# Graph layer with gated update: the second edge bias added by VectorE out of PSUM, the low half taken from SBUF, and x + h summed by GpSimd

## The chip, the core and the metric

The kernel runs on one core of a Trainium2 chip. The metric is the device time of one execution in microseconds. The core has a matrix engine (PE, with its weight loads shown apart as PEld), VectorE (DVE), ScalarE (ACT), GpSimd (POOL) and SyncE (SP). Each of them takes its own instructions strictly in program order; between engines there are only semaphores.

## The reference

`x` is 100000 x 128 (nodes), and there are 50000 edges, sorted by destination, each of one of 4 types.

```python
h = relu(layernorm(x))                                  # per row
for each edge e = (src, dst, t):
    hid = relu(concat(h[src], h[dst]) @ W1[t] + b1[t])  # 256 -> 128
    m   = hid @ W2[t] + b2[t]                           # 128 -> 128, the second edge bias is b2
agg = segment_sum(m, dst)                               # 100000 x 128
gi, gh = agg @ W_ih.T + b_ih, h @ W_hh.T + b_hh         # 3 x 128 each
r, z = sigmoid(i_r + h_r), sigmoid(i_z + h_z)
n = tanh(i_n + r * h_n)
out = x + (1 - z) * n + z * h
```

## The kernel before, in words

The nodes go in 196 groups of 512 rows (128 partitions x 512 columns in the transposed form), the edges in 204 units of 256. One loop of steps, unrolled by 8, does in each step one stage of several units and several groups, so that the work of a step belongs to some ten different units and groups. Every engine has its own function `step(i, m)`, and the order of the calls in it is the order of the instructions on that engine: it is written out by hand. In the steady part each step handles one group of nodes and one unit of edges on every engine.

What a step does around the change:

- **Edges.** POOL gathers the rows of x for both ends (`e_x`, four indirect DMAs a step, L593). ACT normalises them, PE transposes them and multiplies by W1 into bank BE1 (L1455, L1456), ACT adds b1 and applies relu (`e_r`, L1303). PE then makes the messages in the other half of BE1: first a product of a matrix of ones with `b2_rows` (L1468, 256 columns), which puts b2 there, and onto it the two products with W2 (L1472). ACT copies the messages rounded to fp32r into the high half of `e_msg` (L1324, at the end of its step), DVE subtracts that from the bank and writes the low half (`low_half`, L1078), and ACT issues the store of both halves to `messages` in DRAM (`store_messages`, L1251). SP loads windows of 64 message rows for a group of nodes (`n_win`, L544) when the unit five after the group's number has been stored.
- **Sums.** POOL makes the windows' tags relative to the group (`n_rel`, L644), DVE makes selection matrices from them (`n_sel`, L1099), and PE sums the messages with these (L1444).
- **Gates.** PE's products of three passes each (L1364, L1365, L1366) give r, z and n for the group: in a step the products of r (six passes), then those of h_n (three passes into bank BHN), transposes, sums and edges, then those of i_n (three passes), then those of z (six passes), then the messages (L1468, L1472), then four transposes of `n_e` of the group before into bank BHN (L1482). ACT computes `n_r` (L1274), `n_n` (L1311) and `n_zc`, which is 1 - z (L1317, behind the products of z).
- **Output.** DVE forms `n_d` (L1143) and `n_e` (L1150, waits for `n_zc`), PE transposes `n_e` back into BHN, and DVE forms `n_out` (L1088) from bank BHN and `n_xh`. `n_xh` is x + h, made by DVE from `n_h` and `n_x` (L1117).

Three orders matter. On DVE, a step ends with `n_d` and `n_e`, and the next one begins with `n_out`, then `low_half`, then `n_sel`. On PE, the h_n products overwrite bank BHN, which `n_out` reads:

```python
gate(BRZ, 0, s, "ha").then_inc(n_gate_r, 1)
if due(g - 1):
    pe.wait_ge(n_outed, g - 1)
...
gate(BHN, 2, s, "h").then_inc(n_gate_hn, 1)
```

On POOL, a step waits until ACT has normalised an older unit (`e_normed`), moves a word to keep the order (`gate_word`, L599), and issues two gathers, `n_rel` and two gathers; in every fourth step `n_rel` comes ahead of `gate_word`. Steps 20 to 116 have list writes too (L579), three in every fourth step.

Of the kernel before, what the change touches and what calls it, by code (L numbers as in the profile page):

```python
# [12 lines left out]
P = 128  # L13
D = 128
# [75 lines left out]
def gnn_layer(nc, x, edge_rows, dst_cols, dst_flat, types, W1, b1, W2, b2, WihT, WhhT, b_ih, b_hh, out):  # L90
# [22 lines left out]
    with ctx:  # L113
# [30 lines left out]
        b2_rows = sb("b2_rows", [P, TYPES * D], F32R)  # L144
        row_is = sb("row_is", [P, 2])
# [72 lines left out]
        def borrow(buffer, at, width):  # L218
# [18 lines left out]
        b2_two, b2_hi, b2_lo, b2_parts = (  # L237
            e_msg[:].rearrange("p r t w -> p (r t w)")[:, at * TYPES * D:(at + 1) * TYPES * D] for at in range(4))
        b2_two, b2_parts = b2_two.bitcast(F32), b2_parts.bitcast(F32)
# [142 lines left out]
        e_high = sem("e_high")  # L382
        e_low = sem("e_low")
# [172 lines left out]
        def _(pool):  # L556
# [90 lines left out]

            def half_of(i):
# [5 lines left out]
            def step(i, m):  # L654
# [12 lines left out]
                if m % 4 != 2:  # L667
                    relative_tags(i - LAG + 1, m - LAG + 1)
                if within(i, UNITS):
                    gather(i, m, (1,))  # L670
# [16 lines left out]
        def _(dve):  # L687
# [386 lines left out]
            def low_half(i, m):  # L1074
                q, s = i - 10, (m - 10) % UNROLL
                if within(q, UNITS):
                    dve.wait_ge(e_high, q + 1)
                    V.tensor_tensor(e_msg[:, s, :, D:2 * D],  # L1078
                                    bank[BE1][:, message_part].rearrange("p (t d) -> p t d", t=2),
                                    e_msg[:, s, :, 0:D].bitcast(F32), ALU.subtract).then_inc(e_low, 1)  # L1080

            def step(i, m):
                g, s = i - LAG - 2, (m - LAG - 2) % 4
                if within(g, NG):
                    dve.wait_ge(n_back, g + 1)
                    if due(g - 3):
                        dve.wait_ge(n_stored[s], uses(g - 4, s, 4, 16))
                    V.tensor_tensor(n_out[:, s, :], n_xh[:, s, :], bank[BHN][:], ALU.subtract).then_inc(n_outed, 1)  # L1088
                in_head = isinstance(i, int) and i < LAG - 2
                if not in_head:  # L1090
                    low_half(i, m)
                ln_part(i, m, 0)
                g, s = i - LAG + 1, (m - LAG + 1) % 4
                if within(g, NG):
# [5 lines left out]
                    ins.then_inc(n_seled, 1)  # L1100
                ln_part(i, m, 1)
# [13 lines left out]
                if within(g, NG):  # L1115
                    dve.wait_ge(n_normed, g + 1)
                    V.tensor_tensor(n_xh[:, s % 4, :], n_h[:, s % 2, :], n_x[:, s, :], ALU.add).then_inc(n_xhed, 1)  # L1117
# [48 lines left out]
                if isinstance(i, int) and i == CHECK_STEP:  # L1166
                    check_inputs()
                if isinstance(i, int) and i == GENERAL_STEP:
                    general_sums()

# [18 lines left out]
        def _(act):  # L1189
# [77 lines left out]
            def step(i, m):  # L1267
                normalise_edges(i, m, (0, 1))
                g, s = i - LAG, (m - LAG) % 2
# [5 lines left out]
                store_messages(i, m)  # L1275
# [20 lines left out]
                if within(q, UNITS):  # L1296
# [7 lines left out]
                    last.then_inc(e_relued, 1)  # L1304
                g, s = i - LAG, (m - LAG) % 2
# [14 lines left out]
                q, s = i - 9, (m - 9) % UNROLL  # L1320
                if within(q, UNITS):
                    act.wait_ge(e_messaged, q + 1)
# [209 lines left out]
```

## Time and profile before

| | us |
|---|---|
| median of 3 runs | 1748.21 (1745.63 to 1748.54) |
| the profiled execution's own time | 1746.99 |
| its span, first to last instruction | 1745.1 |
| PE busy | 1618.8 (93% of the span) |
| DVE busy | 1645.1 (94%) |
| ACT busy | 1455.9 (83%) |
| POOL busy | 1015.6 (58%) |

The profile is that of one execution. Of matmuls the ends are modelled, so that the start of one to the start of the next says more than a duration. The granted PE clock is 1.000 over the whole span. A row's "idle before, releaser" names what ended the engine's last wait.

### The profile page before, as it was taken

How to read it: one execution, taken by the hardware profiler on the slowest of the kernel's cores; microseconds unless marked ns; L12 is line 12 of the kernel's file. 1: busy time of each engine (PE TensorE's matmuls, PEld its weight loads, DVE VectorE, ACT ScalarE, POOL GpSimd, SP SyncE). 2: the span in 40 equal slices, each digit the busy share in tenths (PEclk: the TensorE clock that was granted, in tenths of full speed). 3: DMA queues.
4: the chain of work that ended last, by engine and by line, in shares of the span. 5: the costliest groups of instructions: out<-in, count | busy, mean ns of one | idle time of the engine just before them, and what ended most of it. 6: DMA issues, size and time to landing. Idle time of an engine off the chain costs nothing.

```text
span 1745.1 us, 43079 instructions
## 1 busy us (share of the span) xinstructions
PE 1618.8 (93%) x10182; PEld 1422.8 (82%) x10182; DVE 1645.1 (94%) x4809; ACT 1455.9 (83%) x3401; POOL 1015.6 (58%) x1343
## 2 busy tenths in 40 slices
PE   0236999999999999999999999999999999999998
PEld 0225888888888888888888888888888888888887
DVE  8997999999999999999999999999999999999986
ACT  0025999999898999999999999999999999999896
POOL 5745666666666666766666555555555655565500
PEclk9999999999999999999999999999999999999999
DMA  2224777777777777777777777777777777777653
GB/s 84 68 61 137 193 203 199 202 199 201 197 203 203 198 201 198 200 199 198 199 197 202 194 199 195 198 197 200 195 202 195 199 199 195 202 192 200 191 142 100
DMA packets 477561, 319.97 MB, mean 183 GB/s; under 512 B 106541, under 2 KB 463629, under 8 KB 477454
## 3 DMA queue, kind: packets, MB, share of 16 engines
q10 hardware_dynamic: 261792, 156.12, 29.1%
q1 hardware_dynamic: 186542, 107.39, 26.2%
q0 software_dynamic: 29120, 55.33, 13.1%
q8 instruction: 30, 0.49, 0.1%
q14 instruction: 77, 0.63, 0.1%
HBM read 212.05 MB, written 106.98 MB: 183 GB/s over the span
## 4 chain that ended last, share of the span: by engine, by line
PE 74%; ACT 0%; issue 0%; DVE 0%; ACTq 0%; DVEq 0%
PE bank L1364 14%; PE bank L1366 13%; PE bank L1365 13%; PE bank L1444 9%; PE bank L1456 4%; PE bank L1472 4%; PE bank L1455 4%; PE bank L1482 4%; PE bank L1434 4%; PE bank L1426 4%; PE bank L1468 1%; ACT n_zc L1317 0%; ACT n_r L1274 0%; DVE n_out L1088 0%; ACT n_h L1226 0%
## 5 line engine op out<-in xcount | busy, mean ns | idle before, releaser
L593 POOL DMA_INDIRECT e_x<-in_x,rows_now x816 | 821.4, 1007 | 247.2 <-issue 239.0
L1209 ACT ACTIVATE e_h<-e_x,shift,rstd 128x128 f32<-128x128 f32 x816 | 355.4, 485 | 103.3 <-DVE shift L1071 65.1
L1226 ACT ACTIVATE n_h<-n_x,shift,rstd 128x128 f32<-128x128 f32 x784 | 385.8, 492 | 0.0
L1364 PE MATMUL bank<-n_h_hi,whh_hi 128*128 128x512 f32 x588 | 248.8, 423 | 1.7 <-ACT n_zc L1317 1.2
L1364 PE MATMUL bank<-n_a_hi,wih_hi 128*128 128x512 f32 x588 | 246.9, 420 | 1.3 <-DVE bank L1111 1.3
L1444 PE MATMUL bank<-n_sel,n_win 128*128 128x256 f32 x1568 | 235.4, 292 | 0.5 <-DVE n_sel L1099 0.5
L1366 PE MATMUL bank<-n_a_hi,wih_lo 128*128 128x512 f32 x588 | 231.9, 394 | 0.0
L1366 PE MATMUL bank<-n_h_hi,whh_lo 128*128 128x512 f32 x588 | 231.7, 394 | 0.0
L1365 PE MATMUL bank<-n_h_lo,whh_hi 128*128 128x512 f32 x588 | 231.5, 394 | 0.0
L1099 DVE TENSOR_SCALAR n_sel<-iota,n_rel 128x256 fp32r<-128x256 f32 x784 | 230.0, 356 | 0.2 <-POOL n_rel L644 0.2
L1365 PE MATMUL bank<-n_a_lo,wih_hi 128*128 128x512 f32 x588 | 229.6, 390 | 0.0
L1274 ACT ACTIVATE n_r<-bank,bsum 128x512 f32<-128x512 f32 x196 | 135.1, 689 | 79.5 <-PE bank L1366 73.7
L1444 PEld LDWEIGHTS bank<-n_sel,n_win 128*128 128x128 f32 x1568 | 198.9, 189 | 2.5 <-DVE n_sel L1099 0.9
L1455 PE MATMUL bank<-e_ht,w 128*128 128x128 f32 x816 | 162.3, 281 | 34.0 <-DVE e_msg L1078 34.0
L1317 ACT ACTIVATE n_zc<-bank,bneg 128x512 f32<-128x512 f32 x196 | 134.8, 688 | 63.5 <-PE bank L1366 53.1
L599 POOL TENSOR_TENSOR gate_word<-g_power 1x1 f32<-1x1 f32 x224 | 46.4, 207 | 228.2 <-issue 107.1
L644 POOL TENSOR_TENSOR n_rel<-n_win,base 128x4 f32<-128x4 f32 x196 | 54.5, 278 | 203.0 <-DMA n_win<-messages 134.6
L1150 DVE TENSOR_TENSOR n_e<-n_d,n_zc 128x512 f32<-128x512 f32 x196 | 135.8, 693 | 37.2 <-ACT n_zc L1317 29.5
L1456 PE MATMUL bank<-e_ht,w 128*128 128x128 f32 x816 | 162.2, 281 | 0.0
L1143 DVE TENSOR_TENSOR n_d<-bank,n_n 128x512 f32<-128x512 f32 x196 | 134.8, 688 | 27.0 <-ACT n_n L1311 23.3
L1455 PEld LDWEIGHTS bank<-e_ht,w 128*128 128x128 f32 x816 | 128.3, 196 | 36.6 <-issue 36.6
L1004 DVE BATCH_NORM_STATS2 bn<-e_x 128x6 f32<-128x256 f32 x408 | 155.1, 421 | 0.0
(179 smaller groups left out, 3842.5 us busy)
## 6 DMA issues: line engine op xcount, KB each, us to landing
n_win<-messages SPq DMA_DIRECT2D x1568, 64.2 KB
messages<-e_msg ACTq DMA_DIRECT2D x204, 257.0 KB, 3.0
n_x<-in_x ACTq DMA_DIRECT2D x195, 256.0 KB
out<-n_out ACTq DMA_DIRECT2D x195, 256.0 KB
e_x<-in_x,rows_now POOLq DMA_INDIRECT x816
rows_now<-lists SPq DMA_DIRECT2D x204, 2.0 KB
lists<-picks,list_rows POOLq DMA_INDIRECT x72
w<-in_W SPq DMA_DIRECT2D x1, 512.0 KB, 5.1
```

The costliest lines, as they stand in the source:

```text
L593: G.indirect_dma_start(e_x[:, s, 2 * end + t, :], None, x, bass.IndirectOffsetOnAxis(ap=rows_now[:, s, t, end:end + 1], axis=0)).then_inc( ...
L1004: return V.bn_stats(bn[:, slot, col:col + 2, :].rearrange("p k c -> p (k c)"), rows.rearrange("p t d -> p d t"))
L1099: ins = V.tensor_scalar(n_sel[:, s % 2, k, :], iota[:], n_rel[:, s % 2, k:k + 1], None, ALU.is_equal)
L1150: V.tensor_tensor(n_e[:, s, :], n_d[:, s, :], n_zc[:, s, :], ALU.mult).then_inc(n_eed, 1)
L1209: last = A.activation(e_h[:, s % 2, k, :], e_x[:, s, k, :], ACT.Relu, scale=rstd[:, slot, col + k:col + k + 1], bias=shift[:, slot, col + ...
L1226: last = A.activation(n_h[:, s % 2, cols], n_x[:, s, cols], ACT.Relu, scale=rstd[:, slot, col + 4 + k:col + 5 + k], bias=shift[:, slot, co ...
L1364: T.matmul(o, w_hi, v_hi, start=start, stop=False, skip_group_check=onto)
L1365: T.matmul(o, w_hi, v_lo, start=False, stop=False, skip_group_check=onto)
L1366: return T.matmul(o, w_lo, v_hi, start=False, stop=stop, skip_group_check=onto)
L1444: last = T.matmul(o, n_win[:, w, k, part_ * D:(part_ + 1) * D], n_sel[:, s, k, :], start=n == 0, stop=n == 3)
L1455: T.matmul(o, w1[:, kind, 0, :], e_ht[:, s, t * P:(t + 1) * P], start=True, stop=False)
L1456: last = T.matmul(o, w1[:, kind, 1, :], e_ht[:, s, (2 + t) * P:(3 + t) * P], start=False, stop=True)
```

## The change

Four things are changed, and the results are the same up to rounding.

1. PE no longer multiplies ones with `b2_rows`; its two products with W2 start the bank themselves.
2. DVE gets an operation `biased` at the end of its step: bank BE1 plus the bias (kept in the new SBUF buffer `b2_two`) into the low half of `e_msg`, in fp32. ACT's copy to the high half reads that buffer in place of the bank and stands later, in the next step behind the first two tiles of `normalise_edges`; DVE's `low_half` now reads SBUF alone and stands behind `n_sel`. The products of the next unit into BE1 wait for `biased` in place of `low_half`.
3. ACT issues the store of the messages behind the relu of the hidden part in place of ahead of `normalise_edges(i, m, (2, 3))`.
4. `n_xh` is made by POOL (`node_sum`), behind `n_rel` in the odd half of the step's gathers, in place of DVE.

```diff
+        b2_two = sb("b2_two", [P, TYPES * D])
...
+            def node_sum(g, m):
+                s = m % UNROLL
+                if not within(g, NG):
+                    return
+                if isinstance(g, int) and g == 0:
+                    pool.wait_ge(n_seled, 1)
+                pool.wait_ge(n_normed, g + 1)
+                if due(g - 3):
+                    pool.wait_ge(n_outed, g - 3)
+                G.tensor_tensor(n_xh[:, s % 4, :], n_h[:, s % 2, :], n_x[:, s, :], ALU.add).then_inc(n_xhed, 1)
...
                 if m % 4 != 2:
                     relative_tags(i - LAG + 1, m - LAG + 1)
+                node_sum(i - LAG + 1, m - LAG + 1)
                 if within(i, UNITS):
                     gather(i, m, (1,))
...
                     dve.wait_ge(e_high, q + 1)
-                    V.tensor_tensor(e_msg[:, s, :, D:2 * D],
-                                    bank[BE1][:, message_part].rearrange("p (t d) -> p t d", t=2),
+                    V.tensor_tensor(e_msg[:, s, :, D:2 * D], e_msg[:, s, :, D:2 * D].bitcast(F32),
                                     e_msg[:, s, :, 0:D].bitcast(F32), ALU.subtract).then_inc(e_low, 1)
...
                     dve.wait_ge(n_back, g + 1)
+                    dve.wait_ge(n_xhed, g + 1)
...
-                if within(g, NG):
-                    dve.wait_ge(n_normed, g + 1)
-                    V.tensor_tensor(n_xh[:, s % 4, :], n_h[:, s % 2, :], n_x[:, s, :], ALU.add).then_inc(n_xhed, 1)
...
+                biased(i, m)
...
+            def biased(i, m):
+                q, s = i - 9, (m - 9) % UNROLL
+                if within(q, UNITS):
+                    dve.wait_ge(e_messaged, q + 1)
+                    first = 2 * ((m - 9) % 2)
+                    V.tensor_tensor(e_msg[:, s, :, D:2 * D].bitcast(F32),
+                                    bank[BE1][:, message_part].rearrange("p (t d) -> p t d", t=2),
+                                    b2_two[:, first * D:(first + 2) * D].rearrange("p (t d) -> p t d", t=2),
+                                    ALU.add).then_inc(e_biased, 1)
...
+                q, s = i - 10, (m - 10) % UNROLL
+                if within(q, UNITS):
+                    act.wait_ge(e_biased, q + 1)
+                    act.wait_ge(e_tagged, q + 1)
+                    A.activation(e_msg[:, s, :, 0:D], e_msg[:, s, :, D:2 * D].bitcast(F32), ACT.Copy).then_inc(e_high, 1)
...
-                store_messages(i, m)
                 normalise_edges(i, m, (2, 3))
...
                     last.then_inc(e_relued, 1)
+                store_messages(i, m)
...
                     if due(q):
-                        pe.wait_ge(e_low, q)
+                        pe.wait_ge(e_biased, q)
...
-                    T.matmul(bank[BE1][:, message_part], ones_r[:], b2_rows[:, first * D:(first + 2) * D],
-                             start=True, stop=False)
                     for t in range(2):
                         o = bank[BE1][:, 2 * P + t * D:2 * P + (t + 1) * D]
-                        last = T.matmul(o, e_r[:, s, t * P:(t + 1) * P], w2[:, first + t, :], start=False, stop=t == 1)
+                        last = T.matmul(o, e_r[:, s, t * P:(t + 1) * P], w2[:, first + t, :], start=True, stop=True)
```

How the instructions stand on DVE from the end of one step into the next, before (the names in brackets are the semaphores waited for; `root` rows are the small steps of the inverse square root, in some steps there and in some not):

```order
L1143 TENSOR_TENSOR n_d<-bank,n_n 128x512 [waits n_ned]
L1150 TENSOR_TENSOR n_e<-n_d,n_zc 128x512 [waits n_back,n_ded,n_zed]
L1061 TENSOR_SCALAR root<-half_var 128x32 [waits ln_vared]
L1088 TENSOR_TENSOR n_out<-n_xh,bank 128x512 [waits n_stored1,n_back]
L1078 TENSOR_TENSOR e_msg<-bank,e_msg 128x2x128 [waits e_high]
L1027 TENSOR_TENSOR root_t<-root 128x32 [waits ln_ops]
L1099 TENSOR_SCALAR n_sel<-iota,n_rel 128x256 [waits n_summed,n_reled]
```

And the same place of the changed kernel, where L1188 is `biased` and L1092 `low_half`:

```order
L1154 TENSOR_TENSOR n_d<-bank,n_n 128x512 [waits n_ned]
L1161 TENSOR_TENSOR n_e<-n_d,n_zc 128x512 [waits n_back,n_ded,n_zed]
L1075 TENSOR_SCALAR root<-half_var 128x32 [waits ln_vared]
L1188 TENSOR_TENSOR e_msg<-bank,b_two 128x2x128 [waits e_messaged]
L1102 TENSOR_TENSOR n_out<-n_xh,bank 128x512 [waits n_stored1,n_xhed,n_back]
L1041 TENSOR_TENSOR root_t<-root 128x32 [waits ln_ops]
L1111 TENSOR_SCALAR n_sel<-iota,n_rel 128x256 [waits n_summed,n_reled]
L1111 TENSOR_SCALAR n_sel<-iota,n_rel 128x256 x3
L1092 TENSOR_TENSOR e_msg<-e_msg 128x2x128 [waits e_high]
```

`biased` now stands between `n_e` and `n_out`, and `low_half` has gone behind `n_sel`.

On PE the messages and what follows them, of the changed kernel (L1491 are the products with W2, L1501 the transposes of `n_e`, L1385 to L1387 the passes of a gate). One row, the product with ones ahead of L1491, is gone; the wait for `n_outed` stands where it stood:

```order
L1387 MATMUL bank<-n_a_hi,wih_lo 128x512
L1491 MATMUL bank<-w,e_r 128x128 [waits e_relued]
L1491 MATMUL bank<-w,e_r 128x128
L1501 MATMUL bank<-ident,n_e 128x128 [waits n_ted,n_eed]
L1501 MATMUL bank<-ident,n_e 128x128 x3
L1385 MATMUL bank<-n_h_hi,whh_hi 128x512 [waits n_zed,n_alo,n_hlo]
...
L1385 MATMUL bank<-n_h_hi,whh_hi 128x512 [waits n_outed]
```

On POOL one step of the changed kernel reads as follows (L659 is `node_sum`); before, the row L659 is not there and the others stand the same:

```order
L601 TENSOR_TENSOR gate_word<-g_power 1x1 [waits l_gated,e_normed,l_loaded1]
L595 DMA e_x<-in_x,rows_now 128x128 x2
L646 TENSOR_TENSOR n_rel<-n_win,base 128x4 [waits n_seled,n_windowed0]
L659 TENSOR_TENSOR n_xh<-n_h,n_x 128x512 [waits n_outed,n_normed]
L595 DMA e_x<-in_x,rows_now 128x128 x2
```

## Rows read from the trace of the kernel before

**Rows 1.** The page: busy time and share of span; the chain that ended last.

```profile
PE 1618.8 (93%) x10182; PEld 1422.8 (82%) x10182; DVE 1645.1 (94%) x4809; ACT 1455.9 (83%) x3401; POOL 1015.6 (58%) x1343
...
PE 74%; ACT 0%; issue 0%; DVE 0%; ACTq 0%; DVEq 0%
```

**Rows 2.** Who waited for whom: us in total, times, longest us.

```profile
ACT n_zc L1317 <- PE bank L1366: 53.1, 156, 0.7
...
DVE n_e L1150 <- ACT n_zc L1317: 29.5, 89, 0.7
...
PEld bank L1364 <- DVE n_out L1088: 9.4, 45, 0.8
```

**Rows 3.** Timeline, one steady step: start us, duration us, engine, line, what.

```profile
1005.35 0.39 PE L1364 MATMUL bank<-n_h_hi,whh_hi 128*128 128x512 f32 x1
...
1010.60 0.39 PE L1366 MATMUL bank<-n_a_hi,wih_lo 128*128 128x512 f32 x1
...
1010.83 0.28 PE L1468 MATMUL bank<-b_rows,ones_r 128*128 128x256 f32 x1
...
1010.95 0.60 PE L1472 MATMUL bank<-w,e_r 128*128 128x128 f32 x4
...
1011.03 0.69 ACT L1317 ACTIVATE n_zc<-bank,bneg 128x512 f32<-128x512 f32 x1 [0.27 <-PE bank L1366]
...
1011.79 0.70 DVE L1150 TENSOR_TENSOR n_e<-n_d,n_zc 128x512 f32<-128x512 f32 x1
...
1012.41 0.68 DVE L1088 TENSOR_TENSOR n_out<-n_xh,bank 128x512 f32<-128x512 f32 x1
...
1013.01 0.41 DVE L1078 TENSOR_TENSOR e_msg<-bank,e_msg 128x256 fp32r<-128x256 f32 x1
...
1013.09 0.39 PE L1366 MATMUL bank<-n_a_hi,wih_lo 128*128 128x512 f32 x1
...
1013.14 0.19 PEld L1364 LDWEIGHTS bank<-n_h_hi,whh_hi 128*128 128x128 f32 x1
...
1013.32 0.39 PE L1364 MATMUL bank<-n_h_hi,whh_hi 128*128 128x512 f32 x1
...
1013.34 1.13 DVE L1099 TENSOR_SCALAR n_sel<-iota,n_rel 128x256 fp32r<-128x256 f32 x4
```

**Rows 4.** Groups by line, DVE: count, busy us, mean ns, idle before.

```profile
L1078 DVE TENSOR_TENSOR e_msg<-bank,e_msg 128x256 fp32r<-128x256 f32 x204 | 85.1, 417 | 9.0 <-ACT e_msg L1324 9.0
```

**Rows 5.** Timeline, POOL's part of the same step.

```profile
1007.24 0.18 POOL L599 TENSOR_TENSOR gate_word<-g_power 1x1 f32<-1x1 f32 x1 [1.49 <-ACT e_h L1209]
...
1010.14 0.21 POOL L644 TENSOR_TENSOR n_rel<-n_win,base 128x4 f32<-128x4 f32 x1
...
1011.77 0.95 POOL L593 DMA_INDIRECT e_x<-in_x,rows_now  x1 [0.31 <-issue]
```

**Rows 6.** Groups by line, POOL: gathers, list writes, and its two wide operations.

```profile
L593 POOL DMA_INDIRECT e_x<-in_x,rows_now x816 | 821.4, 1007 | 247.2 <-issue 239.0 <-DMA n_win<-messages 0.6 <-POOL gate_word L599 0.3
...
L579 POOL DMA_INDIRECT lists<-picks,list_rows x72 | 71.3, 990 | 22.0 <-issue 22.0
...
L560 POOL IOTA n_xh<- 128x816 int32 x1 | 2.2, 2175 | 0.0
L568 POOL IOTA n_x<- 128x512 int32 x1 | 0.5, 544 | 0.0
```

**Rows 7.** Timeline: POOL's word and DVE's sum of two SBUF operands.

```profile
1000.12 0.68 DVE L1117 TENSOR_TENSOR n_xh<-n_h,n_x 128x512 f32<-128x512 f32 x1
1000.12 0.76 POOL L599 TENSOR_TENSOR gate_word<-g_power 1x1 f32<-1x1 f32 x1
```

**Rows 8.** Timeline: store of messages, the windows loaded behind it, and the relu.

```profile
1005.69 0.45 ACTq L1251 DMA_DIRECT2D messages<-e_msg  x1
...
1009.09 5.03 SPq L544 DMA_DIRECT2D n_win<-messages  x8
...
1009.18 0.62 ACT L1303 ACTIVATE e_r<-bank,b_cols 128x128 f32<-128x128 f32 x2
```

More of the change, by code:

```diff
@@ L235, in gnn_layer @@
         descends = borrow(n_zc[:], 0, ECOLS)
-        b2_two, b2_hi, b2_lo, b2_parts = (
-            e_msg[:].rearrange("p r t w -> p (r t w)")[:, at * TYPES * D:(at + 1) * TYPES * D] for at in range(4))
-        b2_two, b2_parts = b2_two.bitcast(F32), b2_parts.bitcast(F32)
+        b2_hi, b2_lo, b2_parts = (
+            e_msg[:].rearrange("p r t w -> p (r t w)")[:, at * TYPES * D:(at + 1) * TYPES * D] for at in range(3))
+        b2_parts = b2_parts.bitcast(F32)
         ends = n_d[:].rearrange("p r w -> p (r w)").bitcast(I32).rearrange("p (k e c) -> p k e c", k=SEGMENTS, e=2)
@@ L382, in gnn_layer @@
         e_high = sem("e_high")
+        e_biased = sem("e_biased")
         e_low = sem("e_low")
@@ L1089, in step @@
                 in_head = isinstance(i, int) and i < LAG - 2
-                if not in_head:
-                    low_half(i, m)
                 ln_part(i, m, 0)
@@ L1100, in step @@
                     ins.then_inc(n_seled, 1)
+                if not in_head:
+                    low_half(i, m)
                 ln_part(i, m, 1)
@@ L1319, in step @@
                 normalise_nodes(i, m, (3,))
-                q, s = i - 9, (m - 9) % UNROLL
-                if within(q, UNITS):
-                    act.wait_ge(e_messaged, q + 1)
-                    act.wait_ge(e_tagged, q + 1)
-                    A.activation(e_msg[:, s, :, 0:D], bank[BE1][:, message_part].rearrange("p (t d) -> p t d", t=2),
-                                 ACT.Copy).then_inc(e_high, 1)
             pipeline(nc, act, LAST, LOOP_END, step)
```

## The prediction

> **What bounds the kernel now.** The page comes first: PE is busy for 93% of the span, DVE for 94%, and the chain that ended last runs over PE for 74% of it [rows 1]. Two engines as full as that leave little room between them, so the list of waits comes next, for those near PE. ACT's `n_zc` waited for the products of z in 156 of 196 groups, DVE's `n_e` waited for `n_zc` in 89, and the weight load of a gate product waited for DVE's `n_out` in 45 [rows 2]. That is a ring: PE, ACT, DVE and PE again. So the last view is the timeline of one steady step, read from one start of the h_n products to the next [rows 3].
>
> The reader is to see that two paths lead from the last pass of z (1010.60) to the next h_n products (1013.32), and that they are equally long. The first is PE's own stream: the bias product at 1010.83, the messages from 1010.95, transposes, six passes of r of which the last starts at 1013.09, and 0.23 us behind it the h_n product, the distance at which a pass follows any other (1010.60 to 1010.83). PE does not pause. The second goes through the other engines: `n_zc` starts 0.43 us after the last pass of z and takes 0.69, `n_e` starts 0.07 after its end, `n_out` 0.62 after the start of `n_e`, takes 0.68, and the weight load of the h_n product starts 0.05 after that (1013.14), 0.18 ahead of the product. The load came right behind `n_out`; it had been held by it. With the 5.25 us from 1005.35 to 1010.60, which belong to both, the second ring is 5.25 + 0.43 + 0.69 + 0.07 + 0.62 + 0.68 + 0.05 + 0.18 = 7.97 us, and a step of PE is 7.97 us too. `n_out` needs the transposes on PE and `n_xh`, but not `n_e`: that it follows `n_e` is DVE's order alone.
>
> **The change part by part.**
>
> *The bias product is removed from PE.* The next product starts 0.12 us behind it (1010.83 to 1010.95) [rows 3], and there are 204 units [rows 4]: 24 us of PE's stream. But it lies between the two ends of the ring's second path, so it shortens the first path alone. If the second is longer, PE reaches the h_n products 0.12 us sooner and waits there. I cost it at nothing; what hides it is the term that follows, and without that it would be worth the 24 us.
>
> *`biased` is added to DVE between `n_e` and `n_out`.* Before, nothing but a small root step stood there. Its nearest row is the old `low_half`, which also reads 256 columns of the bank and as many of SBUF: 0.417 us each [rows 4], but the instruction behind it starts 0.33 us after it (1013.01 to 1013.34) [rows 3], since consecutive instructions overlap. So `n_out` comes 0.33 us later (0.33 to 0.42). It does not wait for the messages on top: their products begin 0.23 us after the last pass of z, while `n_e` is not done before 1.8 us after it. Queued behind it are `n_out` and `n_sel`, and PE waits for both; the first is next. What can be recovered is part of the 0.07 ahead of `n_e`, because DVE reaches it earlier without `n_xh`, and of the 0.18 between load and product: at least 0, at most 0.25 together. A weight load lasts 0.19, which speaks for little room in the 0.18, and a wait for a semaphore must remain of the 0.07, so I take 0.06. That makes a step 0.27 us longer (0.08 to 0.42). Steps 19 to 212 have both a unit whose messages are due and an h_n product behind: 194 x 0.27 = 52 us (16 to 81).
>
> *`n_xh` leaves DVE.* An instruction of 512 columns takes a place of 0.60 us there (1012.41 to 1013.01) [rows 3]; against it stands 0.33 for `biased`, so DVE has 0.27 us a step less to do. It stood between `n_sel` and `n_d`, where DVE will now wait for `n_n` and `n_zc` instead. Worth nothing while `n_e` follows `n_zc`, as it nearly does already.
>
> *`low_half` moves behind `n_sel`, ACT's copy to the next step, the store behind the relu.* `n_sel` follows `n_out` 0.33 us sooner, which cancels the lateness of `n_out` for the sums on PE. The copy stands ahead of `n_r`, whose products end some 0.2 us after the copy can: nothing. The store goes from 1005.69 to the relu's end near 1009.8, and the windows start 3.4 us behind a store and take 5.03 to issue (1009.09) [rows 8]: from about 1013 to 1018. Granting them 3.4 us to land, they are there near 1020.9, and `n_sel` asks for their tags at 1013.34 + 7.97 = 1021.3, later still with longer steps. Nothing, with half a microsecond to spare; beyond that each microsecond would be one of DVE's.
>
> *`n_xh` comes to POOL.* No row shows a wide sum on POOL. From below bounds it a plain fill of 512 columns, 0.54 us; from above the patterned fill of 816 columns, 2.18 us, which for 512 is 1.37 [rows 6]. A sum passes over two operands, each at no more than the plain fill's speed, so I take 1.2. POOL's step runs from 1007.24 to 1012.72 [rows 5], 5.8 us with the usual gap of 0.3 behind it; three list writes in every fourth step of 20 to 116 add 3 x (0.99 + 0.3) / 4 = 1.0 [rows 6]. With the sum that is 7.0, or 8.0 in the steps with lists, against 8.24 for the new ring. It fits, barely.
>
> The Trainium skill speaks against this move: its page "GPSIMD Engine Reference", section "4.1 Engine selection", gives wide sums to VectorE, as GpSimd is about twice as slow with two inputs. By the 4497 ns it states for 2048 columns the sum would be about 1.1 us, an estimate, and the total the same.
>
> *The two engines collide.* POOL's one-element word, which takes 0.18 us [rows 5], took 0.76 when it started with DVE's `n_xh`, and ended 0.08 after it [rows 7]: POOL was held while DVE read two operands from SBUF. The reverse, a long POOL sum holding DVE, has no row. The operations it could hold are `low_half` (now of two SBUF operands), the small root steps, and `n_e`. Where POOL waits for `n_normed`, `n_e` is already running. For the others, 1.2 of 8.24 us is a chance of 15% of a hold of 0.6 us on average, 0.09 a step or 17 us in all; from 0, if the wait on PE covers it, I take 8.
>
> The Trainium skill's page "SBUF — State Buffer", section "Who interferes with whom", states this as a lock: VectorE with two SBUF inputs against a GpSimd instruction that reads SBUF, and whichever comes second is blocked to the end. Rows 7 agree for one direction; by the page the 17 us would stand, and without its other direction 0.
>
> **Sum.** 1746.99 (the profiled execution, whose span is 1745.1 with 1.9 around it) + 52 + 8 = 1807. The median of the runs is 1.2 above that execution, so 1808.
>
> **The rivals.**
>
> *The second path has room after all (faster).* Then the step is PE's own, 0.12 us shorter: 1748 - 24 = 1724. For it speaks that DVE gets 0.27 us a step back and that PE's own recorded wait is tiny. It decides where `n_out` can end 0.27 us sooner than I have it, and the only way is an earlier `n_e`. Against it: `n_zc` starts a fixed 0.43 after PE, and `n_e` starts 0.07 after that is done, so freed DVE time ahead of `n_e` has nothing to start.
>
> *POOL becomes the bound (slower still).* With a sum of 1.4 us, held for 0.7 by `n_e` (the row of 0.70), and waiting in order for the late windows, POOL's step with lists comes to 8.0 + 0.2 + 0.7 = 8.9 us. Its 97 steps would cost 97 x (8.9 - 8.24) = 64 us more: 1872. For it speaks how full POOL is in that part; against it, that POOL's waits can overlap with these holds, and that a longer ring gives it room.
>
> *Nothing measurable* would need losses of exactly the size of a gain; I see no mechanism that fixes it there.
>
> **How the numbers follow.** The forecast has a chance of 0.76, with a range of its own of 1764 (0.08 a step, no collisions) to 1846 (0.42 and 17). The faster rival gets 0.10, POOL 0.11, no change 0.03. The range that leaves out no more than two in ten is 1770 to 1848. About 0.2% (3.5 us) is what can be told from no change: faster 0.10, same 0.03, slower 0.87.
>
> **What the profile of the changed kernel would show.** Right: PE waits for `n_out` ahead of the h_n products in nearly every step, some 0.4 us each (0.27 and the 0.12 of the product that is gone), and the step is about 8.24; `biased` takes about 0.42 and `n_out` starts some 0.95 after `n_e`; `n_e` waits for `n_zc` nearly always; DVE's busy time falls by about 45 us (0.68 less, 0.42 more a step) while the span grows. Wrong: PE without waits there and steps of 7.85 (the first rival), or steps of 20 to 116 longer than those behind them with DVE waiting for `n_rel` (the second). Long root steps or a long `low_half` would show the collision.

## The result, and the profile after it

The changed kernel takes 1985.65 us in the median of its runs (1981.04 to 1990.93), beside 1746.92 us for the kernel before (1744.72 to 1748.54). The ratio is 1.1368, with a 95% interval of 1.1336 to 1.1401: it is slower by 239 us. The forecast was 1808 us and the range 1770 to 1848, so the sign was right and the size was not. The profiled execution has a span of 1989.1 us.

The page of the changed kernel, its span and its line of busy times, which answers to [rows 1]:

```profile
span 1989.1 us, 43203 instructions
...
PE 1713.2 (86%) x9978; PEld 1417.4 (71%) x9978; DVE 1782.7 (90%) x4817; ACT 1522.0 (77%) x3401; POOL 1231.7 (62%) x1539
```

DVE was to lose about 45 us of work and its busy time went up by 138. That is the first sign that DVE's instructions are being held: the same instructions take longer. The groups of instructions on DVE and POOL show which (busy us, mean ns of one, idle ahead of them and for whom):

```profile
L1111 DVE TENSOR_SCALAR n_sel<-iota,n_rel 128x256 fp32r<-128x256 f32 x784 | 340.1, 493 | 59.8 <-POOL n_rel L646 57.5 <-issue 2.3
L1161 DVE TENSOR_TENSOR n_e<-n_d,n_zc 128x512 f32<-128x512 f32 x196 | 135.9, 694 | 62.0 <-ACT n_zc L1344 56.8
L1188 DVE TENSOR_TENSOR e_msg<-bank,b_two 128x256 f32<-128x256 f32 x204 | 87.7, 430 | 2.8 <-PE bank L1491 2.6 <-issue 0.2
L1047 DVE TENSOR_TENSOR root<-root_t,root 128x32 f32<-128x32 f32 x104 | 40.9, 393 | 1.9
...
L659 POOL TENSOR_TENSOR n_xh<-n_h,n_x 128x512 f32<-128x512 f32 x196 | 262.1, 1337 | 103.7 <-ACT n_h L1248 98.8 <-issue 2.4 <-DVE n_sel L1111 1.3
```

In the kernel before, the mean of `n_sel` is 356 ns, 230.0 us in all, and that of this root operation 193. `n_e` is as it was (694 after, 693 before), and `biased` takes 430. POOL's sum takes 1337 ns, where the prediction had 1200.

The list of waits, the answer to [rows 2]:

```profile
POOL n_rel L646 <- DMA n_win<-messages: 265.6, 103, 6.9
ACT n_a_hi L1318 <- PE bank L1465: 129.5, 88, 6.0
PEld bank L1465 <- DVE n_sel L1111: 128.1, 90, 5.3
PEld bank L1385 <- DVE n_out L1102: 116.5, 194, 1.8
POOL n_xh L659 <- ACT n_h L1248: 98.8, 62, 4.5
...
DVE n_sel L1111 <- POOL n_rel L646: 57.5, 53, 4.7
```

The wait for `n_out` now stands in 194 steps, as forecast for the ring. But ahead of it stands a chain that the prediction did not have: `n_rel` waits for the windows, `n_sel` for `n_rel`, PE's sums (L1465) for `n_sel`, and ACT's `n_a_hi` for PE. POOL's wait for the windows does no harm by itself: it was 135 us in 38 steps of the kernel before, where `n_sel` waited for `n_rel` once, for 0.2 us. The wait that tells is that of `n_sel`, here 57.5 us in 53 steps.

Counted from the starts of `n_zc` in the trace, the steps of the kernel before are alike (median 7.98 us, one of 195 over 8.5). Of the changed kernel's, 81 are under 8.5 and 52 over 9.5, up to 12.6. A short step, from one `n_zc` to the next (answers to [rows 3]):

```profile
1206.62 0.69 ACT L1344 ACTIVATE n_zc<-bank,bneg 128x512 f32<-128x512 f32 x1 [0.40 <-PE bank L1387]
1207.34 0.69 DVE L1161 TENSOR_TENSOR n_e<-n_d,n_zc 128x512 f32<-128x512 f32 x1 [0.39 <-ACT n_zc L1344]
1207.95 0.42 DVE L1188 TENSOR_TENSOR e_msg<-bank,b_two 128x256 f32<-128x256 f32 x1
1208.28 0.68 DVE L1102 TENSOR_TENSOR n_out<-n_xh,bank 128x512 f32<-128x512 f32 x1
1209.01 0.19 PEld L1385 LDWEIGHTS bank<-n_h_hi,whh_hi 128*128 128x128 f32 x1 [0.43 <-DVE n_out L1102]
...
1214.82 0.69 ACT L1344 ACTIVATE n_zc<-bank,bneg 128x512 f32<-128x512 f32 x1 [0.30 <-PE bank L1387]
```

This is the predicted ring to the tenth: `n_out` starts 0.94 us after `n_e` (forecast 0.95), the weight load has waited 0.43 (forecast 0.4), the step is 8.20 (forecast 8.24). The missing time is in the long steps. Three kinds of them stand out, and one excerpt of each carries the rest of this document.

**W, a window that lands late.** Same trace: store, windows behind it, and what waits for them.

```profile
1204.68 0.42 ACTq L1273 DMA_DIRECT2D messages<-e_msg  x1
1208.70 5.13 SPq L546 DMA_DIRECT2D n_win<-messages  x8
...
1217.34 0.20 POOL L646 TENSOR_TENSOR n_rel<-n_win,base 128x4 f32<-128x4 f32 x1 [3.09 <-DMA n_win<-messages]
1217.58 2.53 DVE L1111 TENSOR_SCALAR n_sel<-iota,n_rel 128x256 fp32r<-128x256 f32 x4 [0.22 <-POOL n_rel L646]
1217.61 1.28 POOL L659 TENSOR_TENSOR n_xh<-n_h,n_x 128x512 f32<-128x512 f32 x1
1220.16 1.21 PE L1465 MATMUL bank<-n_sel,n_win 128*128 128x256 f32 x8 [1.02 <-DVE n_sel L1111]
```

`n_sel` itself is only 0.22 us late here. But POOL stands in `n_rel` until the windows land, and its next instruction is the sum, which then starts with `n_sel`. The four of `n_sel` take 2.53 us in place of 1.13 [rows 3], and PE waits.

**L, the sum on the root operation.** In two of four steps a root operation stands between `n_e` and `biased`:

```profile
1044.15 0.69 DVE L1161 TENSOR_TENSOR n_e<-n_d,n_zc 128x512 f32<-128x512 f32 x1 [0.62 <-ACT n_zc L1344]
1044.58 1.42 POOL L659 TENSOR_TENSOR n_xh<-n_h,n_x 128x512 f32<-128x512 f32 x1 [1.53 <-ACT n_h L1248]
1044.76 1.29 DVE L1047 TENSOR_TENSOR root<-root_t,root 128x32 f32<-128x32 f32 x1
1045.98 0.41 DVE L1188 TENSOR_TENSOR e_msg<-bank,b_two 128x256 f32<-128x256 f32 x1
```

The sum waits for ACT's `n_h` and so starts while `n_e` runs. `n_e` keeps its 0.69; the small operation behind it takes 1.29 in place of 0.19, and ends with the sum (1046.05 and 1046.00). `biased` and `n_out` are behind it. In the changed kernel 22 of the 96 root operations at this place are held (over 0.6 us), since late windows shift POOL in many steps; in e4 below, with the windows in time, 60 of 96.

**P, a step with list writes on POOL.** POOL's work and `n_sel`:

```profile
1031.30 0.69 ACT L1344 ACTIVATE n_zc<-bank,bneg 128x512 f32<-128x512 f32 x1 [0.40 <-PE bank L1387]
...
1034.90 0.21 POOL L646 TENSOR_TENSOR n_rel<-n_win,base 128x4 f32<-128x4 f32 x1
1035.06 1.27 POOL L659 TENSOR_TENSOR n_xh<-n_h,n_x 128x512 f32<-128x512 f32 x1
1035.15 2.40 DVE L1111 TENSOR_SCALAR n_sel<-iota,n_rel 128x256 fp32r<-128x256 f32 x4 [1.32 <-POOL n_rel L646]
...
1037.61 1.67 PE L1465 MATMUL bank<-n_sel,n_win 128*128 128x256 f32 x8 [1.98 <-DVE n_sel L1111]
...
1043.43 0.69 ACT L1344 ACTIVATE n_zc<-bank,bneg 128x512 f32<-128x512 f32 x1 [0.71 <-PE bank L1387]
```

Here no window is waited for. POOL comes to `n_rel` late from its three list writes, `n_sel` waits 1.32 for it and is then held by the sum as well, and the step takes 12.13 us. Part of that is PE's clock: its granted share was 0.50, the lower of its two levels (1.2 GHz of 2.4), from 1038.5 to 1041.0, right behind its wait of 1.98 us, and 1.00 in a later stretch (1250 to 1280). The eight products of the sums take 1.67 us here and 1.21 in the excerpt of W.

### The profile page after: what moved, and what is told of

Its sections match the earlier page's. It is cut to its first block and busy times, and to the rows that moved or that the text cites. A ratio compares the mean times of both kernels' runs of the same rounds, so it can differ in the third digit from the quotient of the medians.

```text
span 1989.1 us, 43203 instructions
## 1 busy us (share of the span) xinstructions
PE 1713.2 (86%) x9978; PEld 1417.4 (71%) x9978; DVE 1782.7 (90%) x4817; ACT 1522.0 (77%) x3401; POOL 1231.7 (62%) x1539
## 5 line engine op out<-in xcount | busy, mean ns | idle before, releaser
L595 POOL DMA_INDIRECT e_x<-in_x,rows_now x816 | 790.6, 969 | 208.3 <-issue 170.2
L1111 DVE TENSOR_SCALAR n_sel<-iota,n_rel 128x256 fp32r<-128x256 f32 x784 | 340.1, 493 | 59.8 <-POOL n_rel L646 57.5
L1465 PE MATMUL bank<-n_sel,n_win 128*128 128x256 f32 x1568 | 243.1, 299 | 107.2 <-DVE n_sel L1111 106.2
L659 POOL TENSOR_TENSOR n_xh<-n_h,n_x 128x512 f32<-128x512 f32 x196 | 262.1, 1337 | 103.7 <-ACT n_h L1248 98.8
L1385 PE MATMUL bank<-n_h_hi,whh_hi 128*128 128x512 f32 x588 | 270.1, 459 | 38.1 <-DVE n_out L1102 33.0
L1465 PEld LDWEIGHTS bank<-n_sel,n_win 128*128 128x128 f32 x1568 | 203.8, 194 | 129.2 <-DVE n_sel L1111 128.1
L646 POOL TENSOR_TENSOR n_rel<-n_win,base 128x4 f32<-128x4 f32 x196 | 45.0, 230 | 358.2 <-DMA n_win<-messages 265.6
L1385 PE MATMUL bank<-n_a_hi,wih_hi 128*128 128x512 f32 x588 | 251.4, 428 | 6.0 <-DVE bank L1125 6.0
L1387 PE MATMUL bank<-n_a_hi,wih_lo 128*128 128x512 f32 x588 | 233.7, 397 | 0.0
L1387 PE MATMUL bank<-n_h_hi,whh_lo 128*128 128x512 f32 x588 | 231.6, 394 | 0.0
L1385 PEld LDWEIGHTS bank<-n_h_hi,whh_hi 128*128 128x128 f32 x588 | 110.9, 189 | 165.1 <-DVE n_out L1102 116.5
L1318 ACT ACTIVATE n_a_hi<-bank 128x512 fp32r<-128x512 f32 x196 | 117.0, 597 | 130.4 <-PE bank L1465 129.5
L1476 PE MATMUL bank<-e_ht,w 128*128 128x128 f32 x816 | 169.4, 292 | 32.9 <-DVE e_msg L1188 32.9
L1477 PE MATMUL bank<-e_ht,w 128*128 128x128 f32 x816 | 169.5, 292 | 0.0
```

Of the source, the lines that this page charges most:

```text
L595: G.indirect_dma_start(e_x[:, s, 2 * end + t, :], None, x, bass.IndirectOffsetOnAxis(ap=rows_now[:, s, t, end:end + 1], axis=0)).then_inc( ...
L659: G.tensor_tensor(n_xh[:, s % 4, :], n_h[:, s % 2, :], n_x[:, s, :], ALU.add).then_inc(n_xhed, 1)
L1111: ins = V.tensor_scalar(n_sel[:, s % 2, k, :], iota[:], n_rel[:, s % 2, k:k + 1], None, ALU.is_equal)
L1385: T.matmul(o, w_hi, v_hi, start=start, stop=False, skip_group_check=onto)
L1387: return T.matmul(o, w_lo, v_hi, start=False, stop=stop, skip_group_check=onto)
L1465: last = T.matmul(o, n_win[:, w, k, part_ * D:(part_ + 1) * D], n_sel[:, s, k, :], start=n == 0, stop=n == 3)
```

## The experiments

Each ratio is to the kernel before. The theories are W, L, P as above, and R, the ring with `biased` in it. In the expectations of e1, e2 and e4, "theory P" still is POOL's sum as a whole, its time and its hold; in those of e7, e8 and e14 it is POOL's time and its place in order. The mean of list steps (those with list writes in every fourth) is over groups 20 to 95, that of later steps over groups 110 to 189, from the starts of `n_zc`.

### The two halves of the change

**e2** is the change without the fourth part (`n_xh` stays on DVE); **e4** is the kernel before with that part alone.

```diff
# e2, against the changed kernel: POOL
-                node_sum(i - LAG + 1, m - LAG + 1)
# and DVE again
+                    V.tensor_tensor(n_xh[:, s % 4, :], n_h[:, s % 2, :], n_x[:, s, :], ALU.add).then_inc(n_xhed, 1)
# e4, against the kernel before: the same two lines with the signs exchanged
```

> The changed kernel with n_xh made by DVE again, the rest as changed. Theory P: the excess over the ring goes, 1790 to 1830 us. Theory W: the store is as late as before, so most of the excess stays, 1900 to 1960 us (a little less, as POOL reaches n_rel sooner).

> The kernel before with n_xh made by POOL and nothing else changed. Theory P: over 1820 us, with DVE waiting for n_rel or n_sel held. Theory W: the windows come early there, so 1735 to 1760 us, about the kernel before.

e2: 1920.0 us, ratio 1.0956 to 1.105. e4: 1921.4 us, 1.0979 to 1.1016. Against the kernel before of the same round the halves cost 172 and 173 us alone, and together 239: they share part of what they delay. In e2 `n_rel` waits for the windows 473 us in 144 steps and `n_sel` for `n_rel` 115 us in 100, and neither `n_sel` (375 ns) nor the root operations (184 ns) are held: W without L. In e4 it waits 24 us in 11, and the hold is there. Timeline of e4:

```profile
1203.61 1.41 POOL L657 TENSOR_TENSOR n_xh<-n_h,n_x 128x512 f32<-128x512 f32 x1 [0.27 <-ACT n_h L1236]
1203.79 1.28 DVE L1045 TENSOR_TENSOR root<-root_t,root 128x32 f32<-128x32 f32 x1
...
1204.99 0.67 DVE L1101 TENSOR_TENSOR n_out<-n_xh,bank 128x512 f32<-128x512 f32 x1
...
1205.72 0.19 PEld L1374 LDWEIGHTS bank<-n_h_hi,whh_hi 128*128 128x128 f32 x1 [1.24 <-DVE n_out L1101]
```

The mean of this root operation is 678 ns, over 104 of them: 46 are held, to 1.28 us in the median, and the others take 0.19.

### The bias part

**e5** is e2 with the store moved to behind `n_h_hi`; **e6** is e5 with `biased` behind `n_out` and ACT's copy behind `n_r`.

```diff
# e5, against e2
                     A.activation(n_h_hi[:, s, :], bank[BT[s]][:], ACT.Copy).then_inc(n_hhi, 1)
+                store_messages(i, m)
...
                     last.then_inc(e_relued, 1)
-                store_messages(i, m)
# e6, against e5, on DVE (n_out stands between the two places)
-                biased(i, m)
...
+                biased(i, m)
```

> The changed kernel with n_xh on DVE and the store of the messages some 1.7 us earlier, behind ACT's high part of the transposed nodes. If the ring through n_out (theory R, the prediction's step of 8.24 us) and the late windows (theory W) are what the bias part costs, only the ring is left: 1785 to 1815 us. If something else of the bias part costs the time, it stays near the 1920 us of the run with n_xh on DVE alone.

> The run before with the addition of the bias also behind n_out and ACT's copy of the high half behind n_r. R: the ring is as short as in the kernel before, PE's stream is 0.12 us a step shorter, so 1722 to 1745 us, faster than the kernel before. If R is wrong, the same time as the run before, about 1800 us or more.

e5: 1814.3 us, 1.0372 to 1.0409. So the place of the store is worth 106 us in the bias part (`n_sel` waits for `n_rel` once, 4 us, in place of 115 us in 100 steps). What is left is 68 us: R, and what `n_xh` and `biased` together cost DVE. The median step is 8.28 us, and PE's load waits for `n_out` in 188 steps. e6: 1793.8 us, 1.0246 to 1.0287. Taking `biased` off the path gives 20 us back, not 52, so the run misses the range for R and comes near that of its rival. That DVE has no slack there would explain it, but no run shows it alone: with `n_xh` and `biased` both on it, `n_e` waits for `n_zc` in 45 steps for 17 us, less than before the change.

**e3** moves `biased` behind `n_out` in the changed kernel and leaves ACT's copy in its place: 2013.7 us, 1.1494 to 1.1609, above both of its ranges. ACT's copy then waits for `biased` in 203 steps, 198 us in all, ahead of ACT's other work.

> The changed kernel with the addition of the bias behind n_out in place of ahead of it. The ring of the prediction gives steps of 8.24 us wherever nothing else is late; without it these fall to about 7.9, some 100 such steps, so 1950 us if the late steps stay as they are. If the late steps are paced by a path of their own (W, over two steps), what is won in the short steps is lost in the late ones: 1970 to 1990 us.

**e1** puts the store of the changed kernel right behind `normalise_edges(i, m, (2, 3))`:

> The changed kernel with ACT's store of the messages 2.4 us earlier in the step (behind the second pair of edge tiles, not behind the relu). Theory W (the late store makes the windows, n_rel and with them n_sel late): the steps above 8.24 us go, time 1800 to 1850 us. Theory P (POOL's sum of 1.34 us fills POOL and holds n_sel): nearly nothing changes, 1950 to 1985 us.

1983.8 us, 1.1333 to 1.1371: nothing gained, though the windows came in time (41 us in 17 waits). In place of the old wait there is a new one, in e1's list of waits:

```profile
ACT e_ht L1309 <- DVE e_msg L1092: 225.3, 183, 5.8
```

At that place ACT stands in the store's wait for `low_half`, which DVE now runs behind `n_sel`, with `e_ht` and all else behind it. So e1 does not measure W alone; e13 below does.

### What holds DVE

**e7** puts another operation in the sum's place in the kernel before: a word that waits for `n_normed`, then a patterned fill that reads nothing. `n_xh` stays on DVE.

```diff
+                pool.wait_ge(n_normed, g + 1)
...
+                G.iota(scratch[:], pattern=[[1, FILL]], base=0, channel_multiplier=0).then_inc(n_filled, 1)
```

> The kernel before, with DVE making n_xh as always, and on POOL at the place of the changed kernel's sum a word that waits for n_normed and a plain fill of 1280 columns of a scratch tile, some 1.4 us, which reads nothing from SBUF. Theory L (POOL's sum holds DVE's operations that read SBUF, the small root step ahead of n_out and n_sel above all): near the kernel before, 1745 to 1780 us. Theory P (POOL's time and its place in order make the loss): as with the sum on POOL alone, 1880 to 1925 us.

1838.4 us, 1.0508 to 1.0543, between its two ranges. Groups of e7 on DVE:

```profile
L1114 DVE TENSOR_SCALAR n_sel<-iota,n_rel 128x256 fp32r<-128x256 f32 x784 | 276.1, 412 | 38.0 <-POOL n_rel L647 38.0
...
L1076 DVE TENSOR_SCALAR root<-half_var 128x32 int32<-128x32 int32 x52 | 36.6, 704 | 0.1
...
L1048 DVE TENSOR_TENSOR root<-root_t,root 128x32 f32<-128x32 f32 x104 | 19.9, 191 | 0.3
```

The root operation with one operand is held by the fill: 24 of 52 take 1.31 us and the others 0.18 (mean 704 ns). The one with two is not (191), and the 46 of it that ran beside a fill took 0.18. e4's sum holds both (means of 473 and 678). The 92 us go with this hold, that of `n_sel` (412 ns) and P, which no run divides here: list steps average 8.76 us, the later ones 8.19.

The Trainium skill's page "SBUF — State Buffer", section "Who interferes with whom", has both halves: an operation of two SBUF inputs contends with GpSimd's reads, and tensor_scalar can take both of the shared ports and then contends with any GpSimd operation. The trace agrees, 1.31 us against 0.18 beside a fill; in which mode the operation ran, no run here shows.

**e8** is e4 with the sum one group older and right behind POOL's word:

```diff
                 transfers_may_start(i + 1 + 2 * TYPES)
+                node_sum(i - LAG, m - LAG)
...
-                node_sum(i - LAG + 1, m - LAG + 1)
```

> The kernel before with n_xh made by POOL, for a group one older, right behind the word at the start of POOL's step, so that it runs while DVE is at its statistics and not between n_e and n_out. L: most of the 173 us go, 1750 to 1800 us. P: POOL has the same work, 1880 to 1925 us.

1790.4 us, 1.0229 to 1.0263: 131 of the 173 us go with no less work on POOL. `n_sel` is back at 361 ns. The input of the sum is there early, so POOL waits for `n_h` 7 times in place of 165.

The same move in the changed kernel is **e9**; **e10** adds the store behind `n_h_hi`, and **e11** the move of `biased` and the copy as in e6.

> The changed kernel with POOL's sum moved as in the run before: one group older, behind the word. It takes L away from the window between n_e and n_sel and leaves the ring (R) and the late windows (W). If L, W and R act each for itself, 1900 to 1930 us, like the run with n_xh on DVE. If L is what makes the windows late too, 1800 to 1850 us.

> The run before with the store of the messages also 1.7 us earlier: L moved, W taken away, the ring left, and DVE without n_xh. R: steps of 8.24 us and what the moved sum still holds (44 us alone on the kernel before): 1800 to 1845 us.

> The run before with the addition of the bias behind n_out and the copy of the high half behind n_r, so without the ring too. R at the size of the prediction: 40 to 55 us less than the run before, 1755 to 1795 us. If the ring was no bound, the same time as the run before.

e9: 2042.2 us, 1.1641 to 1.1757, above both of its ranges. e10: 1857.8, 1.0609 to 1.0644, above its range. e11: 1859.7, 1.0605 to 1.0667, as its expectation has it for a ring that is no bound. In e9, with late windows (319 us in 110 waits), POOL stands in `n_rel`, the sum, by its new place a step later already, comes later still, and a new wait grows, in e9's list:

```profile
ACT n_zc L1344 <- POOL n_xh L659: 159.4, 49, 4.7
```

The instruction ahead of `n_zc` on ACT is the load of the next `n_x`, which waits for the sum to have read the old one. In e10 that wait is 32 us. That e11 is no better than e10 leaves R unproved there; R rests on the short steps of the changed kernel and of e18. **e12** is e11 with the sum between the first two gathers, waiting for `n_h_lo`:

> The run before with POOL's sum between the first two gathers, waiting for the low part of the transposed nodes, so that it runs beside DVE's two long operations that read PSUM or one SBUF operand. L: the rest of the holds goes, and PE's stream, 0.12 us a step shorter than before, is the bound: 1722 to 1760 us, faster than the kernel before. If the holds were not what was left, the same as the run before.

1958.3 us, 1.1189 to 1.1238, 100 us above e11 and above its range. The wait of `n_zc` for the sum is back at 149 us in 85 steps, and POOL waits 93 us for `n_h_lo`.

### Taking W, L and P out of the change one by one

**e13** is the changed kernel with the store behind `n_h_hi`. **e16** is the changed kernel with the root operation behind `n_out`. **e15** has both. **e14** is e4 with the root operation behind `n_out`.

```diff
# root operation, on DVE (n_out stands between the two places)
-                ln_part(i, m, 7)
...
+                ln_part(i - 1, m - 1, 7)
                 ln_part(i, m, 0)
```

> The changed kernel with one edit: the issue of the message store goes back behind n_h_hi, about where the kernel before has it, instead of behind e_low and the copy. Theory W (late windows: the store moved back by four to five microseconds makes the windows land late, and n_rel, n_sel and TensorE wait for them in turn): n_rel's waits for n_win fall from 266 us to under 150, and the time to 1880 to 1930 us. Rival L (GpSimd's sum holds VectorE's small root operation ahead of n_out, and the late windows only follow from that): the store's place is worth little, 1970 to 1990 us.

> The changed kernel with only the root operation moved behind n_out. If the hold costs by itself and the late windows by themselves, 1930 to 1965 us with n_rel's waits for n_win left above 200 us; if the hold made the windows late, 1850 to 1900 us and n_rel's waits under 150 us; if the hold does not matter once the windows are late, 1975 to 1990 us.

> The changed kernel with both edits, the store behind n_h_hi and the root operation behind n_out. If W and L together are the whole of what the prediction missed, what is left is the ring with biased in it (8.24 us a step): 1810 to 1870 us. If something else costs beside them, it stays above 1890 us.

> The kernel before with the sum of normalised rows and x on GpSimd (as in e4, 1921 us) and, beside it, the small root operation that stands between n_e and n_out moved behind n_out. Theory L (the sum costs because the root operation ahead of n_out is held until it ends, so n_out comes late and TensorE with it): the waits of TensorE's edge passes for n_out fall and the time is 1800 to 1860 us. Rival P (GpSimd's time, not the hold, costs: lists and gathers come late behind the sum): it stays at 1900 to 1930 us.

e13: 1935.8 us, 1.1057 to 1.1097: 50 us less than the change, a little short of the range for W, with `n_rel`'s waits for windows at 42 us in 19 in place of 266 in 103. The store is 1.8 us earlier there (3.77 us ahead of `n_zc` in the median, 1.93 in the changed kernel; not four to five, as the expectation says). At its new place ACT's `n_h` has a wait that it did not have, for `low_half`, of 59 us in 31 steps, so the 50 us are W less what this costs. e16: 1998.1 us, 1.1423 to 1.1475: no gain, above all of its ranges, with the waits for windows left at 293. While windows are late, the hold ahead of `n_out` is rare (22 of 96, as said; 55 of 96 in e13), and taking it away gives nothing. e15: 1885.6 us, 1.0777 to 1.0813: a further 50 us, once the windows are in time. It missed its range, and so did e14 (1864.7 us, 1.0648 to 1.0684; the root operation is worth 57 us there): both kept steps of 10 to 12 us, one in four among the list steps. POOL in such a step of e14, and what follows:

```profile
735.12 1.42 POOL L657 TENSOR_TENSOR n_xh<-n_h,n_x 128x512 f32<-128x512 f32 x1 [1.46 <-ACT n_h L1236]
...
739.22 1.00 POOL L579 DMA_INDIRECT lists<-picks,list_rows  x1 [0.30 <-issue]
...
741.80 0.96 POOL L579 DMA_INDIRECT lists<-picks,list_rows  x1 [0.30 <-issue]
...
745.90 0.22 POOL L644 TENSOR_TENSOR n_rel<-n_win,base 128x4 f32<-128x4 f32 x1
746.05 1.28 POOL L657 TENSOR_TENSOR n_xh<-n_h,n_x 128x512 f32<-128x512 f32 x1
746.16 2.40 DVE L1113 TENSOR_SCALAR n_sel<-iota,n_rel 128x256 fp32r<-128x256 f32 x4 [1.31 <-POOL n_rel L644]
```

From one sum to the next POOL is occupied for 10.93 us, with a step of some 8.3. The first sum has waited 1.46 us for its own step's `n_h`, so POOL could not work ahead.

**e17** is e14 and **e18** is e15, with the three list writes of a fourth step spread over three steps, one each:

```diff
-                    write_half(h)
+                    write_half(h, (i - WRITE_FROM) % WRITE_EVERY)
```

> The kernel before with the sum on GpSimd and the root operation behind n_out (e14, 1865 us), and the three list writes that GpSimd issues in every fourth of steps 20 to 116 spread over three steps, one each. In e14 every fourth step there lasts 10.5 to 12.4 us, the others 8.05 to 8.35. Theory P (in that step the sum, three list writes and four gathers do not fit between two sums, so n_rel comes late, n_sel and TensorE's sums behind it): the long steps go, worth about 24 times 2.5 to 4 us, and the time is 1770 to 1800 us. Rival (the long step has another cause, in n_win or the lock alone): 1845 to 1870 us, with the long steps still there.

> The changed kernel with three edits: the store behind n_h_hi, the root operation behind n_out, and the list writes spread over three steps (e15, 1886 us, with the last added). If P costs in the change what it seems to in e14, the steps of 10 to 12 us go and the time is 1800 to 1840 us, of which 1800 is the ring of 8.24 us a step that the prediction had. If the long steps come from the windows, it stays at 1870 to 1890 us.

e17: 1789.0 us, 1.0219 to 1.0253; e18: 1835.0 us, 1.0472 to 1.0518. Both are in the range of P. The long steps are gone: list steps average 8.22 us in e17 (9.01 in e14) and 8.41 in e18 (8.91 in e15). P is worth 76 us with the sum alone and 51 in the changed kernel. Waits of e18:

```profile
PEld bank L1388 <- DVE n_out L1104: 78.6, 194, 0.8
POOL n_rel L648 <- DMA n_win<-messages: 57.8, 31, 5.8
...
PEld bank L1468 <- DVE n_sel L1114: 32.3, 24, 5.8
```

What is left is the ring: PE waits 0.41 us for `n_out` in each of 194 steps, and the 171 steps of up to 8.6 us average 8.27, where 8.24 were forecast and the kernel before has 8.00. The other 24 steps are 34 us over 8.24 together. In 21 of them ACT's `n_h` waits for `low_half`, as in e13. One of these:

```profile
313.33 1.78 DVE L1049 TENSOR_TENSOR root<-root_t,root 128x32 f32<-128x32 f32 x1
313.75 1.29 POOL L661 TENSOR_TENSOR n_xh<-n_h,n_x 128x512 f32<-128x512 f32 x1
...
316.45 0.48 DVE L1094 TENSOR_TENSOR e_msg<-e_msg 128x256 fp32r<-128x256 f32 x1
...
316.96 0.38 ACTq L1275 DMA_DIRECT2D messages<-e_msg  x1
317.47 0.49 ACT L1250 ACTIVATE n_h<-n_x,shift,rstd 128x128 f32<-128x128 f32 x1 [1.48 <-DVE e_msg L1094]
```

The root operation, now behind `n_out`, is held there too, to the end of the sum. `n_sel` and `low_half` come late behind it, PE waits 1.28 us for `n_sel`, and ACT stands in the store until `low_half` is done, with `n_h` behind it. A root operation is held in 15 of the 24. Windows are hardly in it: `n_sel` waits for `n_rel` in 2 steps of e18.

## Why the prediction was right and where it failed

| Taken out, in this order | us | its share |
|---|---|---|
| changed kernel | 1985.7 | |
| store to behind `n_h_hi` (e13) | 1935.8 | 50, W |
| root operation behind `n_out` (e15) | 1885.6 | 50, L |
| list writes spread (e18) | 1835.0 | 51, P |
| kernel before | 1747.8 | 87, of which R some 52 and the 24 long steps 34 |

The shares belong to this order: W is worth 106 in the bias part alone, and L nothing as long as W is there. They hold what PE's clock adds to long steps, too: the mean granted share is 0.982 in the changed kernel and 1.000 in the kernel before, so at most some 36 us (0.018 x 1989, were PE the bound all along), which no run separates.

**Right: the ring with `biased`.** All its numbers are in the short step above, PE waits for `n_out` in 194 steps as forecast, and in e18 the steps of up to 8.6 us are on average 0.27 us longer than in the kernel before: 52 us over 194 steps, the size of the term. That moving `biased` away gives this back is not shown: e6 gave 20 us and e11 nothing. No run tries the removed product, costed at nothing, by itself.

**Right: the holder, and one of the held.** POOL's sum holds DVE, `n_e` is spared since it is already running, and long root steps show it. `low_half`, also named, is not seen held (424 ns on average). `n_sel`, the costliest of the held, is not in the prediction's list.

**Failed: "For the others, 1.2 of 8.24 us is a chance of 15% of a hold of 0.6 us on average".** The phase is no chance. Where ACT's `n_h` releases the sum, the sum starts during `n_e` (167 of 194 in e4, 66 in the changed kernel), and the instruction behind `n_e` in two of four steps is a root operation on the ring: a hold of 1.1 us in the excerpts, ahead of `biased` and `n_out`. Where POOL is late, the sum is released by `n_rel`, and so is `n_sel`, so they start together: 1.4 us on the way to PE's sums. In 63 of the changed kernel's 196 steps the four of `n_sel` take over 2.2 us. The term of 8 us measured 50 in the change for the first alone, and 57 in e14.

**Failed: "Nothing, with half a microsecond to spare" for the later store.** The sum of times was short. In the excerpt of W it is 4.02 us from the store to the start of the windows' issue (not 3.4), 5.13 for the issue, 3.51 until they have landed and 0.20 for `n_rel`, which had been left out: 12.86 from the store to the end of `n_rel`, where 11.8 were reckoned. (The store itself lands after 3.7 us in the median, 3.0 before, by the two pages.) In e2, with no sum on POOL, that lateness alone costs 106 us: `n_sel` waits for `n_rel` 115 us in 100 steps. In the changed kernel this wait is half as long (57.5 us in 53 steps), but POOL, late in `n_rel`, also pulls the sum onto `n_sel`; that interplay of two of the change's own parts was not in the working.

**Failed: "It fits, barely" on POOL.** The list writes were averaged, 1.0 us a step. They stand in one step of four, all three, and there POOL is occupied for 10.9 us between sums; the prediction's own 5.8 and 1.2 with three writes of 1.29 make as much. The average might have sufficed if POOL could work ahead, but the sum waits for the `n_h` of its own step. e17 and e18 make the average true by spreading the writes, and P goes. The rival "POOL becomes the bound" named the place at a chance of 0.11, with 64 us; P measured 51 to 76, and this rival's sign was there: list steps of 9.42 us on average and later ones of 9.10, with DVE waiting for `n_rel`. As the likeliest case it would have given 1872, still short of W and L.

**Unsettled:** the last 35 us between e18 and the forecast ring (1800) lie in the 24 long steps. Whether the held root operation or ACT's wait in the store sets their length was not separated. ACT's copy, costed at nothing, waits for `biased` in 44 steps of the changed kernel, 79.1 us with one start-up wait of 23.6; no run prices that. No version tried beats the kernel before; the nearest is e17 at 1789.0 us.

## What to carry to other kernels

Two engines that hold each other up can do so in a fixed phase when one semaphore chain releases both, so read from the timeline which instruction is next on the other engine at the moment of release, instead of multiplying a share by a length. Work that comes in one step of four must fit in that step, unless the engine can run ahead; a wait for an input of the same step takes that away. And an instruction put behind a wait on an in-order engine moves with that wait: cost a change's parts together where one part makes late what another part queues behind.

## What the runs showed of the hardware that was not expected

- A 128x32 operation of 0.19 us on DVE took 1.29 us beside a POOL sum of 1.42 (L) and 1.78 beside one of 1.29 (e18), and ended with it both times. Its start was 0.18 us behind the sum's in the first case and 0.42 ahead of it in the second, so why it was the one to wait there is open.
- POOL's fill that reads nothing held a one-operand operation of DVE (1.31 us in place of 0.18, in 24 of 52 cases) and not a two-operand one of the same size (0.18 beside a fill, in 46 cases).
- The sum of two 128x512 fp32 operands on POOL took 1.27 us (e9) to 1.55 (e1) in the mean of a run, and 0.68 on DVE.
